# A cross-attention and feed-forward kernel on one core: another order of preparing the weights

## The reference

```
x = x + attention(layernorm(x), ctx)   # layernorm again inside with gains and offsets; one head
        q = x1 @ Wq + bq; k = x2 @ Wk + bk; v = x2 @ Wv + bv
        softmax(q k^T / sqrt(512)) @ v @ Wo + bo
x = x + ffn(layernorm(x))
        h = x @ (ternary w_fc * row scale).T + gate * (x @ v.T @ fast_b.T @ u.T)
        relu(h)**2 @ (ternary w_proj * row scale).T
```

## Time and profile before

| what | value |
|---|---|
| median of 3 runs | 827.13 us (826.97 to 828.32) |
| the profiled execution, its own time | 828.1 us |
| its span, first to last instruction | 826.3 us |
| TensorE busy | 810.7 us, 98% of the span |
| VectorE busy | 513.7 us, 62% |
| ScalarE busy | 374.2 us, 45% |
| GpSimd busy | 154.4 us, 19% |
| moved by DMA | 36.74 MB |

### The profile page before, as it was taken

The page is one execution under the profiler, slowest core; times in us unless marked ns, Lnnn a source line. Parts: engine busy times, 40 slices in busy tenths (PEclk is TensorE's granted clock), DMA queues, the critical chain, the costliest instruction groups (busy, mean ns, idle before and its releaser), DMA issues.

```text
span 826.3 us, 11141 instructions
## 1 busy us (share of the span) xinstructions
PE 810.7 (98%) x4185; PEld 676.7 (82%) x4185; DVE 513.7 (62%) x1052; ACT 374.2 (45%) x712; POOL 154.4 (19%) x175
## 2 busy tenths in 40 slices
PE   6999999999999999999999999999999999999998
PEld 4678788888888888888888888888888888888886
DVE  5898763676537663676547764586536764477434
ACT  5997463424533263424634254423634255332432
POOL 3241230025001240024100250023300250012001
PEclk9999999999999999999999999999999999999999
DMA  8752010101101011101101011101101010000001
GB/s 319 251 142 98 1 52 1 38 1 52 52 1 39 0 52 52 39 1 51 52 1 40 1 52 51 39 1 50 54 1 39 0 52 1 1 2 25 26 1 51
DMA packets 17485, 36.74 MB, mean 44 GB/s; under 512 B 4596, under 2 KB 4998, under 8 KB 17432
## 3 DMA queue, kind: packets, MB, share of 16 engines
q1 hardware_dynamic: 16868, 34.98, 12.1%
q10 hardware_dynamic: 564, 1.06, 0.3%
HBM read 27.64 MB, written 8.39 MB: 44 GB/s over the span
## 4 chain that ended last, share of the span: by engine, by line
PE 94%; DVE 3%; ACT 1%; DMA 1%; issue 1%; SPq 0%; DVEq 0%; ACTq 0%
PE H L1195 28%; PE O L1175 27%; PE G L1091 24%; PE G L1119 4%; PE H L1201 4%; PE H L1068 1%; PE H L1091 1%; PE G L1148 1%; PE O L1249 1%; PE H L1119 1%; PE H L1050 1%; DMA wring<-in_L_ffn_w_fc_dram 1%; DMA wring<-in_L_ffn_w_proj_dram 0%; PE H L1075 0%; PE H L1060 0%
## 5 line engine op out<-in xcount | busy, mean ns | idle before, releaser
L1195 PE MATMUL H<-xnT,fcT 128*128 128x512 f32 x1024 | 257.4, 393 | 0.0
L1175 PE MATMUL O<-projT,qbuf 128*128 128x512 f32 x992 | 249.0, 393 | 0.0
L1195 PEld LDWEIGHTS H<-xnT,fcT 128*128 128x128 f32 x1024 | 188.3, 188 | 36.8
L1175 PEld LDWEIGHTS O<-projT,qbuf 128*128 128x128 f32 x992 | 183.2, 188 | 36.8 <-DVE qbuf L986 0.3
L717 ACT ACTIVATE qbuf<-rbuf 128x512 fp32r<-128x512 f32 x125 | 78.8, 631 | 124.2 <-PE O L1175 62.4
L986 DVE TENSOR_TENSOR qbuf<-rbuf,qbuf 128x512 fp32r<-128x512 f32 x125 | 93.3, 746 | 64.1 <-ACT qbuf L717 64.1
L982 DVE TENSOR_TENSOR rbuf<-rbuf 128x512 f32<-128x512 f32 x128 | 98.7, 771 | 50.9 <-ACT rbuf L709 49.8
L709 ACT ACTIVATE rbuf<-H,scf 128x512 f32<-128x512 f32 x128 | 87.4, 682 | 80.5 <-PE H L1201 80.3
L570 POOL TENSOR_TENSOR xrs<-xrs,mhalf 128x4 f32<-128x4 f32 x9 | 9.4, 1050 | 347.8 <-DVE xrs L966 347.8
L1091 PE MATMUL G<-n1T,M 128*128 128x512 f32 x276 | 64.2, 390 | 0.2 <-DVE n2T L878 0.2
L1091 PE MATMUL G<-Wvo,tT 128*128 128x512 f32 x270 | 63.9, 389 | 0.2 <-DVE tT L885 0.2
(11 more groups left out here) (169 smaller groups left out, 997.9 us busy)
## 6 DMA issues: line engine op xcount, KB each, us to landing
xb<-in_x_dram SPq DMA_DIRECT2D x8, 1024.0 KB
ctxb<-in_ctx_dram SPq DMA_DIRECT2D x8, 768.0 KB
wring<-in_L_ffn_w_fc_dram SPq DMA_DIRECT2D x16, 256.0 KB, 5.1
wring<-in_L_ffn_w_proj_dram SPq DMA_DIRECT2D x16, 256.0 KB, 3.7
out_dram<-x2a SPq DMA_DIRECT2D x8, 512.0 KB, 2.6
out_dram<-x2b SPq DMA_DIRECT2D x6, 512.0 KB, 2.6
Wq_s<-in_L_xattn_Wq_dram SPq DMA_DIRECT2D x4, 256.0 KB, 4.0
x2a<-in_L_xattn_Wo_dram ACTq DMA_DIRECT2D x1, 1024.0 KB, 9.2
```

What stands on the lines that cost most here:

```text
L1175: mm = pe.matmul(banks[f"O{t}"][:, :], qbuf[:, j % 2, h, t * P:(t + 1) * P], projT[:, j, :], start=(j == 0 and h == HI), stop=(j == NFF - ...
L1195: pe.matmul(banks[f"H{j % 2}"][:, :], fcT[:, k, j * P:(j + 1) * P], xnT[:, h, k, :], start=(k == 0 and h == HI), stop=False)
```

## The change

Only the four strings below differ; no instruction is added or dropped.

- SP: Wk:1, g2row, Wk:0 and Wk:2 come right behind Wq:3, ahead of ring:4. bqrow follows ring:4. Wv comes ahead of ring:6, and ctx behind ring:7.
- PE: the three wkT come right behind wqT:3, the part Wk:1 first; turn:0 and turn:1 follow, then M:0, bq:0, M:1, turn:2, turn:3. Before, bq:0 stood ahead of turn:0, and turn:2 ahead of M:0.
- ACT: vecs and wqT:0 come directly behind abs:0. M:0 stands ahead of tb, and store:2 and abs:5 behind tb and Wo.
- DVE: wkT:1 comes ahead of sides:0, and sides:3 ahead of M:0. bq:0 moves behind M:0, the statistics of x behind bq:0 and ahead of M:1. cs01 goes from ahead of M:0 to behind tern:7.

```
 "sp":
-Wq:1 Wq:0 ring:0 ring:1 ring:2 ring:3 Wq:2 Wq:3 ring:4 Wk:1 Wk:0 g2row bqrow Wk:2 x:0 ring:5 ctx:0 ring:6 ring:7
-Wv:0 ring:8 ring:9 ring:10 ...
+Wq:1 Wq:0 ring:0 ring:1 ring:2 ring:3 Wq:2 Wq:3 Wk:1 g2row Wk:0 Wk:2 ring:4 bqrow x:0 ring:5 Wv:0 ring:6 ring:7 ctx:0
+ring:8 ring:9 ring:10 ...
 "pe":
-wqT:0 wqT:1 vecs wqT:2 wqT:3 bq:0 turn:0 wkT:0 turn:1 wkT:1 wkT:2 turn:2 M:0 M:1 turn:3 wvT:0 wvT:1 n1T:0
+wqT:0 wqT:1 vecs wqT:2 wqT:3 wkT:1 wkT:0 wkT:2 turn:0 turn:1 M:0 bq:0 M:1 turn:2 turn:3 wvT:0 wvT:1 n1T:0
 "act":
-abs:0 abs:1 vecs abs:2 abs:3 wqT:0 wqT:2 wqT:3 store:0 abs:4 store:1 store:2 tb abs:5 Wo M:0 abs:6 abs:7 M:1
+abs:0 vecs wqT:0 abs:1 abs:2 wqT:2 abs:3 wqT:3 store:0 abs:4 store:1 M:0 tb Wo store:2 abs:5 abs:6 abs:7 M:1
 "dve":
-wqT:1 bqacc sides:0 sides:1 sides:2 bq:0 wkT:0 wkT:1 wkT:2 xs01 xs23 cs01 sides:3 M:0 M:1 sides:4 tern:5
-sides:6 tern:7 cs23 n1T:0 n1T:1 M:2 bv:0 ...
+wqT:1 bqacc wkT:1 sides:0 wkT:0 wkT:2 sides:1 sides:2 sides:3 M:0 bq:0 xs01 xs23 M:1 sides:4 tern:5
+sides:6 tern:7 cs01 cs23 n1T:0 n1T:1 M:2 bv:0 ...
```

## The result

The changed kernel takes **835.33 us** (median of 4, 834.64 to 837.59) against 827.35 (median of 4, 826.97 to 828.32): a ratio of 1.0101, with a 95% interval of 1.0089 to 1.0112. It is slower by 1%. The forecast was 835.1. The profiled execution took 834.64, with a span of 832.8: 6.5 us more than the profiled one of before.

What follows compares the result with a forecast made beforehand. TensorE was taken to bound the whole kernel, so early delay reaches the end: 7.2 (wvT:1 late) + 1.3 (slow restart) + 0.4 (cs01) - 0.9 (absorbed) = +8.0 us, from 827.1 to 835.1 us; range 830.7 to 839.5, 8 times in 10.

Steps and rivals of the forecast that it cites:

- the signs named: Expected in the profile: tb beginning at 21.4 to 24 us, M:1's copy near 30, sides:4 at about 31.
- The early transposes: Start of the kernel: wqT:2 at 8.6 us instead of 9.25, abs:3 at 10.25, sides:0 at 12.85, 2.25 us later.
- M:0's start: On TensorE behind turn:1: M:0 begins at 16.7 us instead of 17.51, 0.8 us won.
- M:0's length: On TensorE: 2.7 us at the fast pace, 5.4 at the slow one; the middle, 4.05, was taken.
- P and the queue behind tb: P, POOL's start of tb, at 22.8 us; ScalarE's steps behind it put M:1's copy at 30.1, wvT:1 7.2 us late.
- The restart: TensorE behind its pause ahead of wvT:1: the clock falls, work restarts slowly; 1.3 us, bounds 0 and 3.1.
- cs01: VectorE: 1.01 us of work moved into the stretch from 24 to 60 us; price 0.4 us, bounds 0 and 1.0.
- What the dense stretch absorbs: 24 to 60 us, TensorE, VectorE and ScalarE almost fully busy: their idle time takes 0.9 us off the delay.
- SP: Order of loads: Wv lands earlier and ctx later, but wvT:0 and cs01 come so late that both cost nothing.
- the fast case: M:0 at the fast pace, 2.7 us, ending at 19.4 us; wvT:1 then 5.85 us late.

Runs made afterwards that it cites:

- bq_only: Kernel before with only bq:0 moved behind M:0 on TensorE and VectorE, and tb behind M:0 on ScalarE; 835.41 us, ratio 1.0097.
- sums_first: Changed kernel with abs:5 to abs:7 ahead of tb and store:2 behind M:1 on ScalarE; 832.72 us, ratio 1.0066.
- both_warm: Changed kernel with unused matmuls in TensorE's three long pauses, ahead of wqT:0, wqT:2 and wvT:1; 832.98 us, ratio 1.0073.
- warm: Changed kernel with 80 unused matmuls in TensorE's pause ahead of wvT:1; 834.76 us, ratio 1.0091.
- bq_apart: Changed kernel with bq:0 ahead of the turns on TensorE; on VectorE bq:0 behind sides:2, then the statistics of x, then sides:3 and M:0; 830.82 us, ratio 1.0040.
- changed_again: The changed kernel, unaltered, run once more as reference on another chip; 835.31 us, ratio 1.0108.
- cs_back: Changed kernel with cs01 ahead of M:1 on VectorE instead of behind tern:7; 835.47 us, ratio 1.0097.
- front_only: Kernel before with only vecs and wqT:0 directly behind abs:0 on ScalarE, abs:3 still ahead of wqT:2; 826.90 us, ratio 0.9997.
- early_warm: Kernel before with vecs and wqT:0 directly behind abs:0, plus 20 unused matmuls ahead of each of wqT:0 and wqT:2; 827.68 us, ratio 1.0003.
- loads_only: Kernel before with only the changed order of loads on SP; 830.68 us, ratio 1.0034.
- bq_back: Changed kernel with bq:0 back ahead of the turns on TensorE and ahead of sides:1 on VectorE; 834.15 us, ratio 1.0074.
- tb_late: Changed kernel with tb and Wo behind n1T:1 on ScalarE, and scale:1 and the roots of x ahead of tb on POOL; 838.29 us, ratio 1.0134.

## Why the prediction was right

The kernel is slower by the step that was named: bq:0 behind M:0 makes tb late, ScalarE's queue behind tb makes M:1's copy late, and TensorE's pause lets its clock fall. bq_only shows the first link as sufficient, sums_first the second, both_warm and the rows of warm the third. What the prediction has only in its list of terms, and bq_apart shows, is that tb, Wo, store:2 and the three sums cost ScalarE time between M:0 and M:1 even without the wait for POOL. Of the signs named, tb at 20.60 lies below the band of 21.4 to 24, since M:0 was early and fast; M:1's copy at 28.00 and sides:4 at 29.20 lie 2 us ahead of what was named, and in changed_again they are at 23.55, 30.95 and 32.15. The number is better than some of its terms.

- **The early transposes.** Forecast wqT:2 at 8.6 and abs:3 at 10.25; measured 8.68 and 10.30. sides:0 came at 12.41 instead of 12.85. POOL made the thresholds in 0.7 us where it had taken 1.7 before, when two of its three small instructions lay beside VectorE's bqacc (L933) and took 0.71 and 0.70 us instead of 0.24; the copy of wkT:1 then came last before sides:0.
- **M:0's start.** 16.7 was forecast, 15.78 measured: 0.4 by sides:0, 0.4 by turn:1, which took 0.45 us and not the 0.85 read off other transposes at the slow pace. In changed_again, where turn:1 did take 0.8, it was 16.64.
- **M:0's length.** The middle, 4.05, was taken between 2.7 and 5.4. It was 2.64 in the profiled execution, 4.73 in changed_again, where the pace had not risen when M:0 began, and 3.95 in warm, where the clock had fallen just before and came back during M:0. So values across the bracket occur, and the middle is a mean of executions that differ. That the two groups of times in changed_again differ by M:0's length is likely but not shown, since only one of the five has a profile.
- **P and the queue behind tb.** From M:0's end to tb 2.05 forecast, 2.18 measured; from tb to M:1's copy 7.3 and 7.40; from there to wvT:1 1.36 and 1.33. These carried the sum. wvT:1 is 5.0 us late with the fast M:0 and 8.0 with the slow one; the forecast of 7.2 lay between.
- **The restart.** The granted clock fell in the pause as forecast. 1.83 us were lost until M:2's end, where the term, taken after slack, was 1.3.
- **cs01.** 0.4 was forecast; cs_back shows no price, within its noise.
- **What the dense stretch absorbs.** 0.9 forecast. The 6.9 us at M:2's end became 6.5 at the span's end: 0.4. The start of bv:0 on TensorE (L1060), some 0.5 us behind M:2's end, against the span, kernel by kernel, as differences to before:

| run | bv:0 begins | difference | span | difference |
|---|---|---|---|---|
| before | 28.92 | | 826.3 | |
| front_only | 27.98 | -0.9 | 824.9 | -1.4 |
| early_warm | 28.28 | -0.6 | 825.6 | -0.7 |
| bq_apart | 31.82 | 2.9 | 828.7 | 2.4 |
| loads_only | 31.89 | 3.0 | 828.9 | 2.6 |
| sums_first | 33.52 | 4.6 | 830.9 | 4.6 |
| both_warm | 33.73 | 4.8 | 831.0 | 4.7 |
| bq_back | 35.33 | 6.4 | 833.1 | 6.8 |
| warm | 35.58 | 6.7 | 832.8 | 6.5 |
| changed | 35.78 | 6.9 | 832.8 | 6.5 |
| cs_back | 35.89 | 7.0 | 833.4 | 7.1 |
| bq_only | 37.10 | 8.2 | 834.2 | 7.9 |
| changed_again | 39.66 | 10.7 | 836.7 | 10.4 |
| tb_late | 34.70 | 5.8 | 836.7 | 10.4 |

A delay at that point goes through to the end within 0.5 us, in twelve profiled executions. Only tb_late adds something behind it: wvo:0's wait for Wo and its slow matmuls. That the rest of the preparation absorbs nothing was the prediction's base, and it is the best supported part of it.

- **SP.** That Wv and ctx cost nothing was right for the whole change, but for a reason that was given too lightly: loads_only shows 3.4 us lost to the context's later landing when its reader isn't moved as well.

The sum of the fast case is +6.5 in one profiled execution against another that itself lay 1.0 above its median; the median moved by 8.0. The agreement of 835.1 and 835.33 to 0.2 us is luck in part: the single times of this kernel spread over 4 us. Against the profiled execution the terms were off by +0.9 (M:0's start), +1.4 (M:0's length), +0.4 (cs01), -0.2 (tb's wait and the queue), -0.5 (the restart) and -0.5 (absorption), 1.5 in sum.

What stays open: whether M:0's slow pace would be gone with only the early pauses filled, which no run tried alone, why one of both_warm's five times is 836.05, and what the held comparisons cost by themselves.

## What to carry to other kernels

When a product moves to a later place, follow its consumers to the engine that waits for it in order, and count what stands behind that wait: here 7 us of POOL and ScalarE steps that had lain beside other work came onto the path, though TensorE had everything it needed sooner. Work moved into a wait is free only if its data are there (cs01 and ctx) and if the engine beside it isn't holding it up (tb and the comparisons). A run that moves two steps at once doesn't tell which of them helped (bq_apart). And a stall that is long enough to let TensorE's clock fall costs twice.

## What the runs showed of the hardware

VectorE's comparisons from SBUF (0.48 us for 128x512 float32 to bfloat16) took 1.48 to 1.49 us while POOL multiplied 128x512 tensors, in bq_back (1.43 to 1.45 us a product) and in tb_late (1.26, 1.72 and 1.45); in the changed kernel, beside bn_stats, a product took 1.27. An instruction with two inputs from SBUF (L997) took 1.78 instead of 0.75 in tb_late. It goes the other way too: POOL's 128x4 instructions took 0.70 and 0.71 us instead of 0.24 beside VectorE's L933 in the kernel before. bn_stats, and copies out of PSUM, ran beside the same products at their own length. A small VectorE instruction of 128x4 took 1.01 us instead of 0.17 beside them in the changed kernel.

The clock can fall after a pause of 1.8 us, and when work has already begun again. TensorE and the busy time by stretch, loads_only:

```profile
24.62 0.23 PE L1216 MATMUL O<-identb,above 128*128 128x128 bf16 x1 [1.84 <-DVE below L1002]
...
25.00:26.00 1.00, 1.00 (x11) 0.82 (x9) 1.00 (x4) 0.07 (x1) 0.00 (x0) 0.79 1.05 389
```

TensorE stands still from 22.8 to 24.6 us there, and the granted clock is at 0.79 in the mean of 25 to 26 and at 0.50 from 26 to 28. In warm it fell behind a pause of 1.4 us (13.9 to 15.3): it is at 0.50 from 15.5 on. In bq_back a pause of 3.0 us left it at 1.00. And the profile's clock column stands at 1.00 in the first 20 us of changed_again although M:0 took 4.73 us there instead of 2.64: before the first change that the column shows, only the lengths of the instructions tell the level.
